# Softmax tiles turned by VectorE blocks and SBUF to SBUF transfers in place of TensorE, in an fp32 attention and FFN kernel

## The reference, cut to what matters

```
xn = layernorm(x)
q = xn @ Wq.T (32 heads of 128), k, v = xn @ Wk.T, xn @ Wv.T (8 heads of 128)
q, k = rmsnorm(q) * q_norm_w, rmsnorm(k) * k_norm_w
scores = q k^T / sqrt(128) + bias      # causal mask, and ALiBi: slope of the head x (column - row)
attn = softmax(scores); s = (attn v) @ Wo.T
g = silu((silu(xn Wg^T) * (xn Wu^T)) @ Wd^T)      # inner width 1376
out = x + s * g
```

## Time and profile before

| | |
|---|---|
| median of 3 runs | 2455.03 us (2455.02 to 2456.27) |
| the profiled execution | 2455.46 us, span 2453.7 us, clock 0.998 |
| busy over the span | PE 99%, PE weight load 84%, DVE 69%, ACT 50%, POOL 31% |
| q1 (DMA) | 10.5% of the 16 engines' time |
| a unit | 127.6 us (the loads of `w_o` start 127.6 us apart, at 308.18, 435.81, 563.43 us) |

### The profile page before, as it was taken

One profiled execution on the slowest core, in us unless ns is written; L12 is line 12 of the kernel. 1 busy time (PEld: TensorE's weight loads), 2 busy tenths in 40 slices (PEclk: granted clock), 3 DMA queues, 4 the chain that ended last, 5 costly groups with the idle time before them and its releaser, 6 DMA issues.

```text
span 2453.7 us, 37432 instructions
## 1 busy us (share of the span) xinstructions
PE 2422.6 (99%) x13232; PEld 2070.7 (84%) x13232; DVE 1693.7 (69%) x3788; ACT 1236.1 (50%) x2548; POOL 756.9 (31%) x2053
## 2 busy tenths in 40 slices
PE   7999999999999999999999999999999999999998
PEld 6888888888888888878888888888888888888887
DVE  7777777777778787823377787777777777777132
ACT  4555554555545555543355555555555545545333
POOL 2323231413233323244522232323232314131443
PEclk9999999999999999999999999999999999999999
DMA  3010000000000000023320101010000000010232
GB/s 130 1 40 4 27 18 27 18 27 18 27 18 27 18 27 18 27 91 125 112 78 1 44 1 44 1 44 1 27 18 26 18 27 18 1 44 14 90 103 103
DMA packets 23289, 92.19 MB, mean 38 GB/s; under 512 B 6592, under 2 KB 6720, under 8 KB 19136
## 3 DMA queue, kind: packets, MB, share of 16 engines
q1 hardware_dynamic: 23104, 89.80, 10.5%
HBM read 85.60 MB, written 4.19 MB: 37 GB/s over the span
## 4 chain that ended last, share of the span: by engine, by line
PE 96%; DVE 2%; ACT 1%; issue 1%; POOL 0%; DMA 0%; DVEq 0%; ACTq 0%; POOLq 0%
PE out_ps L401 17%; PE score_ps L377 16%; PE out_ps L414 14%; PE qkv_ps L351 14%; PE ring_ps L388 10%; PE qkv_ps L352 7%; PE score_ps L504 5%; PE qkv_ps L504 4%; PE ring_ps L520 4%; PE ring_ps L359 2%; PE out_ps L520 1%; PE ring_ps L364 1%; PE score_ps L351 0%; DVE y L997 0%; DVE xT_lo L868 0%
## 5 line engine op out<-in xcount | busy, mean ns | idle before, releaser
L597 ACT ACTIVATE pT_hi<-ring_ps 128x512 fp32r<-128x512 f32 x576 | 344.0, 599 | 509.8 <-PE ring_ps L388 497.2
L818 DVE TENSOR_TENSOR pT_lo<-ring_ps,pT_hi 128x512 fp32r<-128x512 f32 x576 | 396.8, 690 | 90.6 <-ACT pT_hi L597 86.0
L589 ACT ACTIVATE probs<-probs,low_min 128x896 f32<-128x896 f32 (+7 forms) x512 | 395.2, 774 | 50.4 <-DVE low_min L810 50.1
L1016 POOL TENSOR_SCALAR rs_x<-sq_sum 128x5 f32<-128x5 f32 x122 | 24.8, 203 | 1128.1 <-DVE sq_sum L749 1128.1
L388 PE MATMUL ring_ps<-ident,probs 128*128 128x128 f32 x2304 | 345.6, 273 | 0.0
L388 PEld LDWEIGHTS ring_ps<-ident,probs 128*128 128x128 f32 x2304 | 281.7, 140 | 42.1
L810 DVE CUSTOM_DVE_ANT_0 probs<-score_ps,rel_sb,slope 128x512 f32<-128x512 f32 (+5 forms) x504 | 301.7, 599 | 5.7 <-PE score_ps L377 4.3
L377 PE MATMUL score_ps<-kv_hi,qT_hi 128*128 128x320 f32 (+4 forms) x760 | 275.6, 363 | 3.0 <-DVE xT_lo L868 2.0
L401 PE MATMUL out_ps<-pT_hi,kv_hi 128*128 128x512 f32 x576 | 265.8, 461 | 2.9 <-DVE pT_lo L818 2.6
L377 PE MATMUL score_ps<-kv_hi,qT_lo 128*128 128x320 f32 (+4 forms) x760 | 261.0, 343 | 0.0
L377 PE MATMUL score_ps<-kv_lo,qT_hi 128*128 128x320 f32 (+4 forms) x760 | 260.3, 342 | 0.0
(11 more groups left out here) (178 smaller groups left out, 5293.5 us busy)
## 6 DMA issues: line engine op xcount, KB each, us to landing
qkv_raw<-w_ffn_dram SPq DMA_DIRECT2D x44, 768.0 KB, 4.2
qkv_raw<-w_qkv_dram SPq DMA_DIRECT2D x15, 1536.0 KB, 6.9
o_raw<-w_o_dram SPq DMA_DIRECT2D x16, 1024.0 KB, 4.8
o_raw<-x_dram SPq DMA_DIRECT2D x4, 1024.0 KB, 6.7
out_dram<-y SPq DMA_DIRECT2D x16, 256.0 KB, 3.7
probs<-x_dram SPq DMA_DIRECT2D x3, 1024.0 KB, 7.9
qkv_raw<-w_qkv_dram SPq DMA_DIRECT2D x4, 384.0 KB, 6.6
probs<-x_dram SPq DMA_DIRECT2D x2, 512.0 KB, 4.8
```

Source lines behind the costliest of these rows:

```text
L589: act.activation(row, row, ACT.Exp, scale=-1.0, bias=low_min[:, i % 2, h, HEAD_CHUNKS[i] - 1:HEAD_CHUNKS[i]], accum_out=row_sum[:, i % 2, ...
L597: act.activation(pT_hi[:, n % SLOTS, :], ring_ps[:, ring_bank(r), :], ACT.Copy).then_inc(ring_high, 1)
L818: dve.tensor_tensor(out=pT_lo[:, n % SLOTS, :], in0=ring_ps[:, ring_bank(r), :], in1=pT_hi[:, n % SLOTS, :].bitcast(F32), op=ALU.subtract) ...
```

## The change

The 36 turns of a unit leave PE. The exponentials are stored in `probs` in an order by 32-column blocks. For each head DVE transposes all 32 x 32 blocks in place (`turn_blocks`), and 16 DMAs a tile, from SBUF to SBUF, carry the blocks (rows of 512 bytes: 4 heads x 32 floats) from quadrant a to quadrant b of the partitions, into `pT_lo`, which has 15 slots now. ACT rounds from there into `pT_hi` (4 slots) and DVE subtracts in place. The products with the reciprocals of the sums are gone: the reciprocals of a tile (128 x 4) go to DRAM in one DMA, come back spread over all partitions (128 x 512) in another, and `scale_att` multiplies the attention output by them. The lag from softmax to `weigh` is two steps now (`LAG = 2`), `out_project` is one later again, and the last unit of a row has 11 steps, not 10. Squares and scaling of q and k are five ACT operations of 128 columns each a tile; their transposes stay on PE, in the bank pair of the projection. The slopes of all units are loaded once. Three PSUM banks serve the scores. The FFN's own third pair of gate/up buffers is gone.

```diff
@@ sync
+            def rec_away(U, i):
+                t = tile(U, i)
+                slot = t % 2
+                alone(rec_done, t)
+                if t > 2:
+                    alone(rec_back[slot], (t - 1) // 2 * 16)
+                sp.dma_start(rec_out_at[slot].rearrange("g p -> p g"), rec[:, i % 2, :], allow_slow_non_contiguous=True).then_inc(rec_out, 16)
+            def turn_probs(U, i):
+                t = tile(U, i)
+                alone(probs_turned, t * G)
+                if t > 2:
+                    alone(weighed, homes_free(U, i))
+                homes = pT_lo[:, HOME_AT[i]:HOME_AT[i] + i + 1, :].bitcast(F32).rearrange("p j (a n) -> p j a n", a=BLOCKS)
+                for a in range(BLOCKS):
+                    for k in range(BLOCKS):
+                        b = (a + k) % BLOCKS
+                        sp.dma_start(homes[b * SQUARE:(b + 1) * SQUARE, :, a], by_chunk[i % 2][a * SQUARE:(a + 1) * SQUARE, 0:i + 1, b]
+                                     ).then_inc(probs_back[t % 2], 16)
+            def rec_home(U, i):
...
@@ tensor, step
+                if not (last and i >= TILES - 2):
+                    project(U + (i + 2) // TILES, (i + 2) % TILES, first and i + 2 < TILES)
+                if not (last and i >= TILES - 1):
+                    turn_qk(U + (i + 1) // TILES, (i + 1) % TILES, first and i + 1 < TILES)
...
+                if not (first and i <= LAG):
                     out_project(U, i)
+                for k in range(sooner, chunks):
+                    scores(U, i, k, first)
...
+                    V, p = U - (i < LAG), (i - LAG) % TILES
+                    for j in range(p + 1):
+                        weigh(V, p, j, None if first and i == LAG else U * TILES + i - LAG)
@@ scalar, step: the order
+                        high_att(U, i)
+                    for j in highs[:HIGH_SLOTS // 2]:
+                        high_probs(V, p, j)
+                        scale_qk(N, n, first and n)
+                    for j in highs[HIGH_SLOTS // 2:HIGH_SLOTS]:
+                        high_probs(V, p, j)
...
+                        high_q(N, n, first and n)
+                            high_k(N, n, first)
+                        squares(U + (i + 2) // TILES, (i + 2) % TILES, first and i + 2 < TILES)
+                        stage_v(U + (i + 2) // TILES, (i + 2) % TILES, first and i + 2 < TILES)
...
@@ vector
+            def turn_blocks(U, i, h):
+                dve.wait_ge(exped, (tile(U, i) - 1) * G + h + 1)
+                row = by_head[i % 2][:, h, 0:(i + 1) * BLOCKS, :]
+                dve.transpose(row, row).then_inc(probs_turned, 1)
+            def low_probs(U, i, j):
+                n = TURN_AT[i] + j
+                dve.wait_ge(probs_high, U * TURNS + n + 1)
+                dve.tensor_tensor(out=home(i, j), in0=home(i, j).bitcast(F32), in1=pT_hi[:, n % HIGH_SLOTS, :].bitcast(F32),
+                                  op=ALU.subtract).then_inc(probs_low, 1)
+            def scale_att(U, i):
+                t = U * TILES + i - LAG
+                dve.wait_ge(weighed, (t - 1) // TILES * TURNS + TURN_AT[(t - 1) % TILES + 1])
+                dve.wait_ge(rec_back[t % 2], ((t - 1) // 2 + 1) * 16)
...
@@ vector, step: the order
+                        scale_att(U, i)
+                    for j in lows[:1]:
+                        low_probs(V, p, j)
+                        low_att(U, i)
+                    for j in lows[1:HIGH_SLOTS]:
+                        low_probs(V, p, j)
+                    lows = lows[HIGH_SLOTS:]
...
+                        low_q(N, n, first and n)
+                            low_k(N, n, first)
...
                         add_y(U, i, first)
+                    for k in range(sooner, chunks):
+                        bias(U, i, k)
+                        h, part = divmod(k, HEAD_CHUNKS[i])
+                        if part == HEAD_CHUNKS[i] - 1 and h >= 2:
+                            turn_blocks(U, i, h - 2)
...
+                        for h in (G - 2, G - 1):
+                            for j in lows[:1]:
+                                low_probs(V, p, j)
+                            lows = lows[1:]
+                            if h == G - 1:
+                                reciprocals(U, i)
+                            turn_blocks(U, i, h)
+                    for j in lows:
+                        low_probs(V, p, j)
```

More of the change, by code:

```diff
@@ L51 @@
 TURNS = TILES * (TILES + 1) // 2
[L52 to L65, removed]
-LAG = 2
[L69 to L88, removed]
+TURN_AT = [i * (i + 1) // 2 for i in range(TILES + 1)]
+BLOCKS, SQUARE = 4, 32
+LAG = 2
+HIGH_SLOTS = 4
+HOMES = 2 * TILES - 1
+HOME_AT = [HOMES - 1 - i if i % 2 else 0 for i in range(TILES)]
+PER_TURN = BLOCKS * BLOCKS * 16
+SBANKS = 3
+assert SCORES % SBANKS == 0 and TURNS % HIGH_SLOTS == 0
 def build(nc, x, w_qkv, w_o, w_ffn, q_norm, k_norm, rel, slopes, inv_slopes, ident_in, out):
@@ L330, in _, with project @@
         def _(pe):
[L331 to L341, removed]
+            def project(U, i, first):
+                t, acc = tile(U, i), acc_of(i, first)
+                if not (first and i < 3):
+                    pe.wait_ge(qk_low, 2 * (t - 2))
                 for c in range(DC):
@@ L441, in step @@
-                if first and i == 1:
-                    pe.wait_ge(qk_done, tile(U, 2))
-                    pe.wait_ge(v_staged, tile(U, 2))
-                elif not (last and i >= TILES - 2):
-                    project(U + (i + 2) // TILES, (i + 2) % TILES, qkv_ps, False)
-                late = last and TILES - 2 <= i <= TILES
-                spread = i == 1 and not first
-                if spread:
-                    out_project(U, i, range(0, 2))
-                elif not (first and i < 2) and not late:
-                    out_project(U, i)
@@ L527, in chunk @@
                         return
-                    gate_up(c, k, half, range(1, 2) if c == 1 else range(2))
+                    gate_up(c, k, half)
                     down(c - 1, 1 - k)
@@ L697, in unit @@
+                    if first and i == 0 and U == 0:
+                        for t in range(HT, HT + 2):
+                            high_x(0, t)
+                    for j in highs:
+                        high_probs(V, p, j)
+                    if i == TILES:
+                        high_gate_up(0, 0)
+                        high_down(0, 0)
+                    if i == TILES + LAG:
+                        high_gate_up(1, 1)
+                        high_down(1, 1)
                 def unit(U, first, last):
@@ new lines, in step @@
+                    if first and i == 0:
+                        early_norms(tile(U, 2))
+                    if first and i == 1 and U == 0:
+                        for t in range(HT + 2, TILES):
+                            low_x(0, t)
+                    if not (last and i >= TILES - 1):
+                        low_q(N, n, first and n)
+                        if n:
+                            low_k(N, n, first)
+                    chunks = G * HEAD_CHUNKS[i] if i < TILES else 0
+                    sooner = 2 if last and i == TILES - 2 else 0
@@ new lines, in step @@
+                    if i == TILES - 1 and not last:
+                        low_k(U + 1, 0, False)
+                    if first and i == 0 and U == 0:
+                        for t in range(HT, HT + 2):
+                            low_x(0, t)
+                    if i < TILES:
+                        for h in (G - 2, G - 1):
[5 more added lines that the diff above has]
+                            turn_blocks(U, i, h)
@@ L970, in unit @@
-                    for i in range(TILES + 2 if last else TILES):
+                            dve.wait_ge(rel_in, 16)
+                    for i in range(TILES + LAG + 1 if last else TILES):
                         step(U, i, first, last)
```

651 lines of the change are left out of this document (291 added, 360 removed).

## The result

The changed kernel takes 2584 us (median of 4 runs, 2578 to 2589) against 2455 (2455 to 2456): ratio 1.052, 95% interval 1.050 to 1.055. Slower, inside the range, but 123 us over the time named. The sign, too, had only 0.51.

A forecast was written before the change was run, and what follows sets the result against it. PE's instruction list bound the kernel before; after, waits for DVE would take back nearly all the gain. From 2455.46 us, -18 for 16 units (126.5 against 127.6) and +24 for row ends gave 2461.5, named 2461; range 2330 to 2610.

The forecast's parts named there:

- The sign: Whole kernel: slower than before, with a chance of 0.51, against 0.42 for faster and 0.07 for the same.
- PE's list and the turns: PE's instructions a unit: 36 turns of 0.44 us, 15.8 us, go out, leaving a list of some 111 us.
- The block transposes: DVE's 32 transposes a unit: 0.10 us + 1.05 ns a column, 0.70 us in the mean, 22.6 us a unit.
- Rivals 1 and 3: DVE's block transposes: at 0.52 ns a column 2361 us, chance 0.21; at two cycles an element 2742 us, chance 0.10.
- The port: DVE's low halves with two SBUF inputs and POOL's operations exclude each other: 0.4 us a unit, bound 13.
- Rival 4: The port is held between DVE and POOL: 6.5 us a unit, 2565 us; chance 0.09.
- The lists of steps 2 to 7: DVE's loops bound these steps: 12.8 to 20.2 us each, 1.5 to 3 us over PE's list.
- The row ends: Deeper pipe at the start and end of each row: 12 us a row, 24 us in all, bounds 0 and 50.
- The clock: PE in the attention: all instructions priced at the full 2.4 GHz, with no term for a slower clock.
- The transfers: SBUF to SBUF moves of each tile: 512-byte rows at 32 ns, hidden; cover gone from some 50 ns a row.
- A quarter of the DMA engines' time: DMA engines: the share of their time said to be in use, with 1.5 MB and 1 MB loads queued behind a tile.
- Rival 2: Tile transfers land late: at 80 ns a 512-byte row, 7 us a unit more, 2577 us; chance 0.10.

The follow-up runs named there:

- e11: Changed kernel without the reciprocals' way through DRAM: neither transfer issued, `scale_att` using a constant tile; 2507 us.
- e4: Changed kernel with the reciprocals sent out as 128 rows of 16 bytes instead of 512 of 4, coming back in another order; 2514 us.
- e7: Changed kernel without the tiles' transfers and without the block transposes on DVE; 2340 us.
- e2: Changed kernel without the 16 transfers of every tile; the reciprocals' way through DRAM stays; 2498 us.
- e9: e5 with the reciprocals turned by one more block transpose and sent out as 16 rows of 128 bytes; 2460 us.
- e1: Changed kernel with four transfers a tile in place of 16, same bytes and 512-byte rows; 2532 us.
- e5: Changed kernel with the five scalings of q and k first in ACT's step, ahead of `high_att` and two `high_probs`; 2494 us.
- e3: Changed kernel with the reciprocals' transfer out issued behind a tile's 16 transfers, not ahead of them; 3176 us.
- e6: Changed kernel with reciprocals as 128 rows of 16 bytes and their order followed through by strided operations, output the reference's; 2593 us.
- e8: Changed kernel with e5 and e6 together, output the reference's; 2521 us.

## Why the prediction was right in sign and 123 us short

The sign was forecast with a chance of 0.51, little more than a coin's. It rests on more than the term that failed, though: without the rows of 4 bytes the time is still 2507 to 2514 us (e11, e4). The steps, one by one:

- **PE's list and the turns: good to 2 us.** In e7, where PE hardly waits, it is busy 113.7 us of a unit's 117.0, for a list of 111.8. PE's share of a unit's window came out at 92% (e2, and the shorter unit above), not 87: by busy time, which counts a matmul longer behind a wait and at half clock.
- **The block transposes: right.** 1233, 1098, ... 300 ns for 1024, 896, ... 128 columns, against 0.09 + 0.10 us + 1.05 ns a column (1265 at 1024). Rivals 1 and 3 fall:

```profile
L797 DVE STREAM_TRANSPOSE probs<-probs 128x1024 f32<-128x1024 f32 x64 | 78.9, 1233 | 0.0
L797 DVE STREAM_TRANSPOSE probs<-probs 128x128 f32<-128x128 f32 x64 | 19.1, 300 | 0.3
L809 DVE TENSOR_TENSOR pT_lo<-pT_lo,pT_hi 128x512 fp32r<-128x512 f32 x576 | 397.2, 704 | 265.3 <-ACT pT_hi L578 264.7
```

- **The port: as counted.** The low halves take 704 ns in the mean against 690 before: 36 x 0.014 is 0.5 us a unit, where I had 0.4. Rival 4 (6.5 us a unit) falls.
- **The lists of steps 2 to 7: right.** Without the transposes (e7) a unit is 117.0 us for lists that gave 116.5. In e2, at the full clock, steps 2 to 6 come within 0.2 us, step 7 0.4 us long, steps 0 and 1 0.6 and 0.7. PE's waits lie where I put them (q and k, then `pT_lo`).
- **The row ends: mis-sized, 24 us where 42.5 came.** PE's first `out_project`, the last of row 1 and the first of row 2, in the kernel before and in e2 (start, us):

```profile
53.28 0.40 PE L414 MATMUL out_ps<-o_hi,attT_hi 128*128 128x512 f32 x1
...
1058.40 0.39 PE L414 MATMUL out_ps<-o_hi,attT_hi 128*128 128x512 f32 x1
...
1267.72 0.40 PE L414 MATMUL out_ps<-o_hi,attT_hi 128*128 128x512 f32 x1
```

```profile
77.47 0.50 PE L408 MATMUL out_ps<-o_hi,attT_hi 128*128 128x512 f32 x1
...
1085.89 0.39 PE L408 MATMUL out_ps<-o_hi,attT_hi 128*128 128x512 f32 x1
...
1312.41 0.51 PE L408 MATMUL out_ps<-o_hi,attT_hi 128*128 128x512 f32 x1
```

  24.2 us at the first start, 17.2 between the rows (226.5 less 209.3), some 1 at the end. The first steps hold little of PE's work to cover the deeper pipe, and I gave them 4 us.
- **The clock: a term put at nothing.** The attention between these marks takes as long as before (2011 against 2010 us in both rows), where I had 18 less. I priced every list at the full clock. At the full clock e2's unit is 125.7 us, 0.8 less than my 126.5; the half clock brings the mean to 127.4. Of the 18.5 us, 15 are the 0.9 a unit; the other 4 lie in steps outside those 14 units.
- **The transfers: the step that failed.** I wrote "Hidden; the cover is gone from some 50 ns a row", and priced 512 bytes at 32 ns. The price was good: without rows of 4 bytes beside them the rows cost 34.5 ns in the mean (e4, e9, e11). The threshold, meant for rows that are all slow, wasn't tested: in the changed kernel the median is 33 and the mean 60. What failed is the sentence after: "The 4-byte rows of the reciprocals go ahead of the last transpose, in its shadow." I priced their issue and their bytes and not what they do to the rows beside them, of the tile behind and of the tile before, nor how long they take to land. Ahead of a tile they cost 70 us through stragglers; behind it, 592 more. SP's pace, which I took from two loads 0.44 us apart, is 0.65 for these, and stayed mostly hidden. Of the remaining 16 us (e4 over e2) the trace says where they lie: at the full clock e4's steps are e2's within 0.2 us, but seven steps 0 and nine steps 3 have a stretch at 0.50, where e2 has three and four, and these cost 1.4 to 3.7 us each. What sends the clock down there no run shows. "A quarter of the DMA engines' time" was the transfers alone: without stragglers the queue has 42% (e4), since 10.5% was there before and the reciprocals come home as 256 KB a tile (19% in e2, which has no transfers).

In sum: 2461, + 37 (row ends 18.5, units and their clock 18.5), + 16 (transfers), + 70 (rows of 4 bytes) = 2584. The last two are what came back in this order of taking things away; e1 shows that they aren't independent. Rival 2's 2577 holds rows that all take 80 ns and row ends of 24 us where 42.5 came, so its place was right and its number luck. It had 0.10, because I took 80 ns a row for far-fetched by the 32 and looked for no other way in which rows get slow. The mechanism of the straggling itself stays open (whether the 4-byte writes to DRAM hold something that the rows need, and what). Shown is when it happens: every row over 1 us starts 1.4 to 11.7 us after such a batch of 4-byte rows has begun, in all three kernels that have them beside a tile, which is about the time that the batch takes to land. And it comes and goes with them: 2702, 5454 and 2259 rows over 1 us in the changed kernel, e1 and e5, which have them ahead of a tile; 1 in e3, which has them behind; 0 in e4, e6 and e8 to e11, which have none.

The Trainium skill ("DMA: Bandwidth & Descriptors", Rules for kernel authors) says that a strided last dimension becomes one descriptor an element and should be made contiguous; by that rule, the trace agrees (512 rows of 4 bytes a tile); the price lay with the transfers next to them.

## What to carry to other kernels

Ask of each small strided DMA what is in flight beside it, ahead and behind, until it has landed: 2 KB in rows of 4 bytes held up the 2 MB of tile 7, and one small block transpose, which made the rows 128 bytes, was far cheaper. On an in-order queue, where a small transfer stands decides who waits for it. When work moves off the bounding engine, write the order of every engine anew: two reorderings that cost nothing (scalings ahead of the waits, low halves ahead of transposes) gave 90 us (72 in e8) and 22 us; with the longer rows they turned the change from 5% slower into 0.7% faster.

## What the runs showed of the hardware

- 512 rows of 4 bytes to DRAM (2 KB) are through the DMA engines within 1 us and land 7.6 to 12.4 us after their issue (median 8.9), behind a tile's 512-byte rows (e3) or with none about (e2). Rows that run in that time straggle up to 6.4 us in the changed kernel, while the DMA engines are 0.11 to 0.23 busy.
- SP issues SBUF to SBUF transfers of 32 partitions some 0.65 us apart, whatever their size (16 in 10.5 to 10.9 us in the mean for each of the tiles 0 to 7 in e4), against 0.44 between two loads.
- Part of PE's idle time is paid twice, by the clock that falls after it. PE's busy time for the same 10928 instructions grows as its waits do: 2216 us in e7 (span 2337, mean clock 0.986), 2265 in e2 (2497, 0.975), 2297 in the changed kernel (2579, 0.962), 2419 in e3 (3173, 0.882). Between e2 and the changed kernel that is 32 us, beside the 82 by which their spans differ; how much of it delayed the end isn't shown. The time at 0.50 is 12 us in the kernel before, 67 in e7, 127 in e2, 162 in e4, 199 in the changed kernel, 748 in e3.
